# Counting edges by pairs of 14-destination groups, ten tiles a turn, with the codes laid out by GpSimd

## The reference

```python
edge_index = jnp.stack([src, dst])
xn = _layernorm(x, axis=-1)
x = x + _L0_gnn_ref(xn, edge_index, edge_type_3, ...) + _L0_mix_ref(xn[None], ...)[0]
x = x + _L0_ffn_ref(_layernorm(x, axis=-1)[None], ...)[0]

# in the graph attention, per layer
alpha = jax.nn.leaky_relu(qi + kj, 0.2)
m = jax.ops.segment_max(alpha, dst, ...); e = jnp.exp(alpha - m[dst])
a = e / (jax.ops.segment_sum(e, dst, ...)[dst] + EPS)
out = jax.ops.segment_sum(a[:, :, None] * oj.reshape(...), dst, ...)

# in the linear attention
qf = _phi(q); kf = _phi(k)                       # x + 1 where x > 0, else exp(x)
kv = jnp.einsum('bhnd,bhne->bhde', kf, v); y_num = jnp.einsum('bhnd,bhde->bhne', qf, kv)
y = y_num / jnp.maximum(y_den, EPS)              # y_den = qf . sum of kf
```

## Time and profile before

| | us |
|---|---|
| median of three runs | 1674.98 |
| lowest, highest | 1670.88, 1675.16 |
| the profiled execution | 1673.72 |
| its span, first to last instruction | 1672.0 |
| busy in the span: TensorE, VectorE | 1574.0, 1313.5 |
| busy: ScalarE, GpSimd | 809.4, 144.4 |

### The profile page before, as it was taken

How to read it: one execution, slowest core, us unless ns; L and a number is a source line. 1 busy time by engine, 2 the same in 40 slices (tenths; PEclk the granted TensorE clock), 3 DMA queues, 4 the chain that set the end, 5 groups by cost and what they waited for, 6 DMA issues and landing times.

```text
span 1672.0 us, 34410 instructions
## 1 busy us (share of the span) xinstructions
PE 1574.0 (94%) x10567; PEld 1139.5 (68%) x10568; DVE 1313.5 (79%) x2633; ACT 809.4 (48%) x1074; POOL 144.4 (9%) x280
## 2 busy tenths in 40 slices
PE   5899998988999999999999999989999999999987
PEld 4566675666556666699999999976555555555544
DVE  7699968989489999288898998972774577777795
ACT  6331115552235664378888888962222233333352
POOL 3000000000100000000000000000000143333340
PEclk9999998999999999999999999989999999999998
DMA  6111115520456663540132033023766521101212
GB/s 208 37 60 59 60 48 175 165 81 29 133 190 217 201 199 115 177 131 31 62 94 62 31 115 118 14 89 98 210 204 187 203 79 56 53 3 56 89 38 93
DMA packets 129294, 178.54 MB, mean 107 GB/s; under 512 B 15509, under 2 KB 100606, under 8 KB 129202
## 3 DMA queue, kind: packets, MB, share of 16 engines
q1 hardware_dynamic: 129202, 177.38, 33.7%
HBM read 120.47 MB, written 56.88 MB: 106 GB/s over the span
## 4 chain that ended last, share of the span: by engine, by line
PE 71%; issue 15%; DVE 7%; ACT 2%; DMA 2%; DVEq 1%; POOL 0%; SPq 0%; POOLq 0%; ACTq 0%
PE ps L2219 23%; PE ps L2173 14%; PE ps L2279 7%; PE ps L2278 7%; PE ps L1993 4%; PE ps L2084 3%; PE ps L1980 2%; PE ps L1981 2%; PE ps L1982 2%; DVE oh_q L1472 1%; PE ps L2290 1%; PE ps L2156 1%; DVE oh_p L1473 1%; PE ps L2036 1%; ACT q_m L1092 1%
## 5 line engine op out<-in xcount | busy, mean ns | idle before, releaser
L2219 PE MATMUL ps<-xrh,pf 128*128 (+1 forms) x2400 | 399.0, 329 | 4.8 <-DVE pf L1758 4.8
L2219 PEld LDWEIGHTS ps<-xrh,pf 128*128 128x128 f32 x2400 | 392.5, 190 | 11.2 <-issue 9.0
L1980 PE MATMUL ps<-w_hi,xt_hi 128*128 128x384 f16 x600 | 197.6, 329 | 10.0 <-DVE ev_t L1507 3.4
L2278 PE MATMUL ps<-x,ph 128*128 (+1 forms) x600 | 195.2, 325 | 11.8 <-POOL pl L991 11.8
L1758 DVE SCALAR_TENSOR_TENSOR pf<-vb,CT 128x1260 f32<-128x1260 f32 x118 | 172.8, 1468 | 33.6 <-PE ps L2219 33.6
L1981 PE MATMUL ps<-w_lo,xt_hi 128*128 128x384 f16 x600 | 197.4, 329 | 0.0
L1982 PE MATMUL ps<-w_hi,xt_lo 128*128 128x384 f16 x600 | 197.2, 329 | 0.0
L2279 PE MATMUL ps<-x,ph 128*128 (+1 forms) x600 | 196.5, 328 | 0.0
L1472 DVE TENSOR_SCALAR oh_q<-pat,codeT,neg_w 125x630 f16<-125x630 uint16 x420 | 185.0, 441 | 13.8 <-PE ps L1993 7.7
L1754 DVE SCALAR_TENSOR_TENSOR vb<-vb,tb 128x1260 f32<-128x1260 f32 x118 | 170.0, 1466 | 12.7 <-ACT vb L1226 11.8
L1666 DVE CUSTOM_DVE_ANT_0 tt_junk<-kbc,mb 126x1260 bf16<-126x1260 f32 x120 | 169.1, 1466 | 11.7 <-issue 11.7
(11 more groups left out here) (266 smaller groups left out, 2359.1 us busy)
## 6 DMA issues: line engine op xcount, KB each, us to landing
qbc<-tq_d SPq DMA_DIRECT2D x12, 1260.0 KB, 6.5
wst<-in_L_gnn_W SPq DMA_DIRECT2D x60, 192.0 KB, 3.2
xr_d<-ev SPq DMA_DIRECT2D x60, 192.0 KB, 2.0
x_d<-ev SPq DMA_DIRECT2D x60, 192.0 KB, 2.4
mb_d<-mb SPq DMA_DIRECT2D x30, 310.1 KB
mb<-mb_d SPq DMA_DIRECT2D x30, 310.1 KB
xrh<-xr_d SPq DMA_DIRECT2D x3, 2880.0 KB, 15.5
x<-x_d SPq DMA_DIRECT2D x2, 3840.0 KB, 18.1
```

Source lines behind the costliest of these rows:

```text
L1980: pe.matmul(ps[:, bank, 0:CW], a_hi, hi[:, k, :], start=(k == 0), stop=False)
L2219: mm = pe.matmul(out[b], pf[j][:, b * DB:b * DB + P], x, start=(first and b % 2 == 0), stop=False, skip_group_check=True)
L2278: pe.matmul(ps[:, bank, 0:CW], p, cols(off, off + CW), start=start, stop=False, skip_group_check=True)
```

## The change

The windows become 14 destinations wide, 90 of them, and are counted as 45 **pairs**. A window's columns are 10 x 3 x 14 = 420, one matmul and one PSUM bank a tile, and the pair's two windows have a bank each. A turn is ten tiles at fixed places: places 0 to 4 belong to the pair's first window, 5 to 9 to its second. Nothing is done outside the loop; TensorE clears the two banks by two matmuls of two columns ahead of it. The places are handed over in groups of 4, 3 and 3 (`UNITS`).

VectorE no longer finds the tile's codes at an address worked out from the table: GpSimd copies them, for a turn ahead, to one of four places of `cw` (codes less the window's offset, five tiles an operation) and `sw` (sources). `codes_of` does this: two loads of table words, a loop over the turns, and in a turn four operations on 125 x 5. VectorE's `oh_q` so has one per-partition scalar, not two; it waits for `cw_done` and gives a place back by `cw_free`, which starts three ahead.

The table has two parts, the tiles of 90 windows and the turns of 45 pairs; they are stored by two transfers with 2 and 4 bytes a line. A pair's counts are copied out and stored as 840 columns. K has ten pairs, V twenty, three follow, and each query block has two (`QW = 2`): one at its fourth step, whose one-hots VectorE makes at the end of the block before, and one at its end, whose one-hots follow `wt_lo` of the third step. The attention has none. Later steps use three windows of 14 where they had two of 21 (masks, `sel`, `kbc2`'s nine loads for six).

```diff
-WN = 21
+WN = 14
-TF = 4
-TM = 3
-TG = TF + TM
+TT = 5
+TG = 2 * TT
+UNITS = ((0, 4), (4, 7), (7, 10))
+RR = 4
...
-        QW = 3
-        W_A = W_Q + QW * K6
+        QW = 2
+        assert W_Q + QW * K6 == NWP and WT_TILES == K6 * K6
...
-            sp.dma_start(tab_d.rearrange("o w -> w o"), tabi[:, :]).then_inc(tab_io, 16)
-            sp.wait_ge(tab_io, 16)
-            sp.dma_start(tabrow[:, :], tab_d[:, :]).then_inc(tab_io, 16)
+            sp.dma_start(tab_d[0:1, 0:NTAB].rearrange("o w -> w o"), tab16[:, 0:1]).then_inc(tab_io, 16)
+            sp.dma_start(tab_d[0:1, NTAB:2 * NTAB].rearrange("o (w c) -> w (o c)", c=2), tab16[0:NTAB // 2, 1:3]).then_inc(tab_io, 16)
+            sp.wait_ge(tab_io, 32)
+            sp.dma_start(tabrow[:, :].bitcast(U16), tab_d[:, :]).then_inc(tab_io, 16)
...
+            def codes_of(w):
+                tiles = pool.value_load(tabrow[0:1, ds(w, 1)], min_val=0, max_val=(NT - 1 << 16) + NT - 1)
+                count, first = window(pool, w)
+                tile0 = (pool.snap(tiles & 65535, min_val=0, max_val=NT - 1), pool.snap(tiles >> 16, min_val=0, max_val=NT - 1))
+                with pool.Fori(0, count) as jj:
+                    n1 = pool.snap(first + jj + 1)
+                    o = pool.snap(n1 & (RR - 1), min_val=0, max_val=RR - 1)
+                    pool.wait_ge(cw_free, n1)
+                    for u in range(2):
+                        t = pool.snap(tile0[u] + TT * jj)
+                        t = pool.snap(NT + (t - NT) * (t < NT))
+                        t = nc.s_assert_within(t, 0, NT, skip_runtime_bounds_check_because="a tile past the last is held at NT")
+                        pool.tensor_tensor(cw[0:ET, ds(o, 1), TT * u:TT * u + TT].rearrange("p o n -> p (o n)"), codeT[0:ET, ds(t, TT)],
+                                           neg_w[0:ET, ds(2 * w + u, 1)].to_broadcast([ET, TT]), ALU.add)
+                        last = pool.tensor_copy(sw[0:ET, ds(o, 1), TT * u:TT * u + TT].rearrange("p o n -> p (o n)"), sloT[0:ET, ds(t, TT)])
+                    last.then_inc(cw_done, 1)
+            pool.wait_ge(tab_io, 48)
+            with pool.Fori(0, W_Q) as w:
+                codes_of(w)
             pool.wait_ge(qk_ready, 64)
             pool.tensor_scalar(qkn[:, :, :, :], qkn[:, :, :, :], SPLIT, None, ALU.mult).then_inc(qk_ready, 1)
...
             pool.tensor_copy(bsplit[:, 2, :], bcol[:, :]).then_inc(bf_step, 1)
+            with pool.Fori(W_Q, NWP) as w:
+                codes_of(w)
...
-                dve.tensor_scalar(oh_q[0:ET, u, :], pat[0:ET, :], codes[:, k:k + 1], neg_w[0:ET, ds(w, 1)], ALU.subtract, ALU.is_equal)
+            def one_hots(count, first):
                 with dve.Fori(0, count) as jj:
                     n1 = dve.snap(first + jj + 1)
+                    o = dve.snap(n1 & (RR - 1), min_val=0, max_val=RR - 1)
+                    dve.wait_ge(cw_done, n1)
+                    for i in range(len(UNITS)):
+                        dve.wait_ge(oh_free[i], n1)
+                        for k in range(*UNITS[i]):
+                            a = dve.tensor_scalar(oh_q[0:ET, k, :], pat[0:ET, :], cw[0:ET, ds(o, 1), k:k + 1].rearrange("p o n -> p (o n)"), None, ALU.is_equal)
+                            b = dve.tensor_scalar(oh_p[0:ET, k, :], iota_l[0:ET, :], sw[0:ET, ds(o, 1), k:k + 1].rearrange("p o n -> p (o n)"), None, ALU.is_equal)
+                        b.then_inc(oh_rdy[i], 1)
+                    a.then_inc(cw_free, 1)
...
-                    if k in (1, 3, 4)[:QW - 1]:
-                        count_part(wa + (1, 3, 4).index(k) + 1)
+                    if k == 2:
+                        count_part(wa + 1)
...
-                count_part(wa + QW)
+                if more:
+                    count_part(wa + QW)
...
-                for w in block_windows(i):
-                    if w + 1 < NWN:
-                        count_part(w + 1)
...
+                for u in range(2):
+                    pe.matmul(ps[:, bank + u, 0:2], ident16[:, :], zrow[:, 0:2], start=True, stop=False, skip_group_check=True)
                 with pe.Fori(0, count) as jj:
                     n1 = pe.snap(first + jj + 1)
-                    pe.wait_ge(oh_rdy[2], n1)
-                    for u in range(TF, TG):
-                        last = tile(u, False)
-                    last.then_inc(oh_free[2], 1)
+                    for i in range(len(UNITS)):
+                        pe.wait_ge(oh_rdy[i], n1)
+                        for k in range(*UNITS[i]):
+                            last = pe.matmul(ps[:, bank + k // TT, 0:QN], oh_p[0:ET, k, :], oh_q[0:ET, k, :], start=False, stop=False, skip_group_check=True)
+                        last.then_inc(oh_free[i], 1)
...
-                        if k in (2, 4, 5)[:QW - 1]:
-                            u = (2, 4, 5).index(k)
-                            count_window(wa + u, 6, *of_w[u])
+                        if k == 3:
+                            count_window(wa, 6, *of_w[0])
```

More of the change, by code:

```diff
@@ L186, in build @@
         oh_q = place("oh_q", [P, TG, QN], F16, 190720)
[L187 to L189 removed]
+        oh_p = place("oh_p", [P, TG, P], F16, 199136)
+        cb = [place(f"cb{j}", [P, 2 * QN], U16, 185344 + 1696 * j) for j in range(2)]
+        cc_ = [place(f"cc{j}", [P, 2 * QN], U16, 141312 + 1696 * j) for j in range(2)]
+        cw = place("cw", [P, RR, TG], F32, 173056)
+        sw = place("sw", [P, RR, TG], F32, 173248)
+        tabrow = place("tabrow", [1, NTAB], I32, 173440)
         ev = [place(f"ev{j}", [P, CW], F32, 67584 + 1536 * j) for j in range(2)]
@@ L657, in _ @@
                 for u in range(QW):
-                    for t in ((0, 1), (2, 3), (4,), (5,))[u] if QW == 4 else ((0, 1), (2, 3), (4, 5))[u]:
+                    for t in range(3 * u, 3 * u + 3):
                         wq_load(6 * q + t + 6)
@@ L781, in _ @@
             sp.wait_ge(kq_st, 32)
-            for u in range(2):
+            for u in range(WU):
                 for r in range(R):
@@ L1466, in _ @@
                     pair_low(p - 1)
[L1467 removed]
+            for i in range(len(UNITS)):
                 dve.sem_inc(oh_free[i], 1)
[L1470 to L1482 removed]
+            dve.sem_inc(cw_free, RR - 1)
+            def one_hots(count, first):
                 with dve.Fori(0, count) as jj:
                     n1 = dve.snap(first + jj + 1)
[L1485 to L1490 removed]
+                    o = dve.snap(n1 & (RR - 1), min_val=0, max_val=RR - 1)
[7 more added lines that the diff above has]
+                    a.then_inc(cw_free, 1)
             def w_lo_part(c):
@@ L1500, in count_part @@
             def count_part(w):
[L1501 removed]
+                one_hots(*window(dve, w))
             def k_sum(c, n, j):
@@ L1960, in table_sums @@
                 pe.wait_ge(e_row, 6)
-                pe.wait_ge(e_const, 1)
-                pe.matmul(ps[0:NTAB, 0, 0:1], ltri[:, :], tab[:, 1:2], start=True, stop=True).then_inc(e_tr, 1)
+                pe.wait_ge(e_const, 2)
+                for c in range(2):
+                    last = pe.matmul(ps[0:NTAB // 2, 0, c:c + 1], ltri[:, c, :], tab[:, 1:2], start=(c == 0), stop=(c == 1), skip_group_check=True)
+                last.then_inc(e_tr, 1)
             for p in range(NB // 2):
@@ L2024, in _ @@
                         w = W_K + (c - 1) * NB + 2 * ii + j
-                        _, count, first = window(pe, w)
+                        count, first = window(pe, w)
                         pe.wait_ge(g_free, n + 1)
@@ L2122, in _ @@
                     weighted(i + 1)
-                for w in block_windows(i):
-                    count_window(w, 6, *window(pe, w)[1:])
                 if i < 2:
```

180 lines of the change are left out of this document (75 added, 105 removed).

## The result

The changed kernel takes 1700.02 us (median of four, 1694.52 to 1700.73), the kernel before 1674.97: a ratio of 1.0148, 95% interval 1.0122 to 1.0175. It is slower by some 25 us; the forecast was 1671.6, its range ended at 1688. The profiled execution is the fastest of the four, 1694.52 with a span of 1692.8. Against the profile of before the span grew by 20.8, and that is what can be followed; the other three executions, 5 to 6 us above it, have no trace.

A forecast was written before the change was run, and what follows sets the result against it. VectorE was taken to bound the attention, TensorE K and V, a chain between them Q. Terms +3 + 0 + 5.3 + 1 - 2.4 - 9 = -2.1 took 1673.72 to 1671.6 us; range 1657 to 1688.

The forecast's parts named there:

- The time of a one-hot: VectorE's tile: oh_q some 325 ns long, a start every 0.245, 0.405 us a tile and 4.06 a turn.
- TensorE's share of a turn: Ten matmuls of 420 columns, 1.98 us, and two clearing matmuls: about the 2.08 of before, so nothing gained.
- the 2.4 us at the attention's start: Start of the attention: block 0's rdn no longer waits for the count, -2.4 us.
- the pace of a block at full clock: Attention block without a window: 4.6 us at full clock, at most 4.45 if nothing lies between.
- the mechanism at the start of Q: Start of query blocks: codes wait behind GpSimd's splits, delaying one-hots, then wt_lo, then TensorE; +5.3 us.
- the price of a scalar: VectorE's oh_q: dropping one of two per-partition scalars saves 57 ns, giving 0.303 at 630 columns and 0.243 at 420.
- the rival of the hold-up: Slower rival: GpSimd's four operations a turn hold up VectorE's one-hots, 0.76 us longer a turn; about 1703 us, chance 0.10.
- the first stretch: Before K: second table store priced at its 0.48 issue, plus GpSimd's first turn and a longer first turn; +3 us.
- K to S: K, V and the three windows after: VectorE's 0.45 us more a turn fits its idle time; 0, from -1 to +6.
- +0.2 a block: Query blocks: chain from last QF to last QF 19.35 us against 19.07; +1 over five blocks.
- The attention: -9 taken: Attention blocks without windows take 5.0 us instead of 6.0 over nine intervals: -9, from -3.6 to -14.
- the costlier tile: Slower rival: one-hot at 0.276, a turn 4.36 us, +12, 1684; costlier tile or turn has chance 0.14.

The follow-up runs named there:

- the run with the third store: Changed kernel with a small third store of 8 two-byte elements put between the table's two stores and their load; 1697.06 us.
- The new order: Changed kernel with each query block's two counts placed behind the second and fourth wt_lo of that block on VectorE; 1674.72 us.
- the added products: Changed kernel with table row by TensorE, early codes, reordered query counts, plus nine useless products per attention block; 1652.38 us, 0.9877 to the kernel before.

## Why the prediction was wrong

*Right.* The time of a one-hot (324 ns, 4.01 us a turn), TensorE's share of a turn, the 2.4 us at the attention's start, the pace of a block at full clock (4.47), the mechanism at the start of Q, and that GpSimd's operations would not hold up VectorE's. The one-hot's size is no evidence for the price of a scalar by which it was found: 0.36 x 420/630 = 0.24 gives the measured distance without one, and no run takes the two edits apart. The Trainium skill's rule (SBUF — State Buffer, Who interferes with whom) names two cases. That a VectorE instruction with two SBUF inputs contends with a GpSimd instruction that reads SBUF agrees with the trace: in the rows above it is GpSimd's that lasts 2.97 us instead of 0.2. The case of the two-port modes, which the prediction set beside the rival of the hold-up, decides nothing here: no one-hot was held up, and no trace shows in which mode they ran.

Every stage but one came out dearer than forecast: of the 23 us between the sum of -2.1 and the +21.1 measured, 9.7 lie in the first stretch, 5.4 from K to S (the three windows behind V), 1.8 at the start of Q, 4.5 in Q and 1.9 in the attention.

*The step that failed: the first stretch.* "Bounds +1.5 and +5, I take +3": it was +12.7. I priced the second store by its issue, 0.48. The 6.5 us from the store to its load stand nowhere in the sum, that is they were put in as unchanged; I had no row for a column of 2-byte elements, and should have kept them as a unit that can double. The stores took 8.0 us more, and with the load's landing 8.8. GpSimd's first turn cost 2.6 (from the words' arrival to the first one-hot 3.7 instead of 1.1), about as forecast, and the longer turn 0.4. The last 1.0 is TensorE's clock between the first product of K and the end of the window, 0.63 instead of 0.74. It doesn't go with the longer idle time ahead of it: in the run with the third store the same stretch took 6.2 us, behind 14.44 idle.

*The second: Q.* "The chain has not become shorter. +0.2 a block": it was 1.1. I read the blocks' pace as a chain through the first count and TensorE's four steps, and left the second count beside it; but that count waits for the first window on TensorE and stands ahead of the fourth `wt_lo`, so the chain runs over both counts: 0.8 + 4.0 + 0.9 + 1.9 + 1.3 + 4.0 + 0.9 + 1.9 + 4.4 = 20.1 (issue, count, `wt_lo`, a step of TensorE, its window until places come free, count, `wt_lo`, a step, the closing window with `QF`). The new order shows it: without either count in the chain, 17.7.

*Sizes.* At the start of Q the term was +5.3 and it was +7.1: from the end of the splits to the first one-hot it takes 3.2 us (269.44 to 272.63), not 1.05. The loads and register steps of GpSimd alone take 2.0; in its first stretch the prediction itself had given loads and operations together 1.4 to 2.3 and the register steps. K to S: 0 taken, -1 to +6 given, +5.4 measured, of which VectorE's longer turn has 3.7 in V: of its 8.0 us more there nearly half came through, although 9.8 had been idle. The attention: -9 taken, -7.1 measured, 5.2 us a block instead of 5.0; the clock decided it, as the added products show.

The rival that came nearest in time, the held-up one-hots (1703), had the wrong cause, as had the costlier tile (1684): that 1703 lies by the measured 1700 is chance. What I lacked was a rival in the place where I knew least: a wait on a transfer at the front, which nothing covers. TensorE was already idle there for 3.4 us, so each microsecond more was on the path from the first.

## What to carry to other kernels

A small transfer through memory that engines wait for is a serial latency of its own kind: look at what waits for it before changing its shape, and if the data are a column in SBUF, a product with the identity makes the row without it. When work moves to an engine that stood aside, its queue decides: find the chain that the new instructions now stand behind. And a count of what is saved on an engine tells nothing until the chain from one block to the next is written down with each piece in the queue's order; moving the same counts to other places in VectorE's queue was worth 17.6 us in Q and at its start, and all that the change saved in the attention was 9.5.

## What the runs showed of the hardware

Storing a column of 96 elements of 2 bytes took 11.5 us from issue to the end of the wait, of 4 bytes 5.8, and 48 to 96 elements of 4 bytes differed by 0.5. Work without use on TensorE, some 1.5 us a block (an estimate: nine products whose starts lie 0.163 us apart at full clock) in time that it would have idled, shortened nine blocks from 49.2 to 39.6 us: with TensorE idle for 1.3 to 2.2 us ahead of each block's transposes the granted clock went back and forth between its two levels, 1.2 and 2.4 GHz, with 0.5 to 0.7 from the second block on it stayed at 1.00. An operation of GpSimd with 125x5 elements that takes 0.2 us alone took 2 to 4.6 beside VectorE's large operations with two inputs in SBUF, while VectorE's didn't wait.
